# A four-network graph kernel: last attention summed by blocks and sources, GpSimd's low parts in halves, first products read in PSUM, one later spread

## The reference

```
def gat_layer(x, W, a_s, a_d, b, edge_index, concat):
    h = (x @ W).reshape(n, H, C)
    alpha_s = jnp.einsum('nhc,hc->nh', h, a_s)
    alpha_d = jnp.einsum('nhc,hc->nh', h, a_d)
    e = jax.nn.leaky_relu(alpha_s[src] + alpha_d[dst], NEG_SLOPE)
    m = jax.ops.segment_max(e, dst, num_segments=n)
    e = jnp.exp(e - m[dst])
    denom = jax.ops.segment_sum(e, dst, num_segments=n)
    msg = h[src] * (e / (denom[dst] + EPS))[:, :, None]
    return jax.ops.segment_sum(msg, dst, num_segments=n) + b
...
x = _layernorm(x + _L0_gnn_ref(x, ...), axis=-1)
```

## Time and profile before

| what | us |
|---|---|
| median of 3 runs | 1843.94 (1842.36 to 1847.01) |
| the profiled execution | 1845.62 |
| its span in the trace | 1843.8 |
| PE busy | 1777.4 (96%) |
| DVE busy | 1226.3 (67%) |
| ACT busy | 718.9 (39%) |
| POOL busy | 701.7 (38%) |

### The profile page before, as it was taken

One profiled execution on the slowest core, in us unless ns is written; L12 is line 12 of the kernel. 1 busy time (PEld: TensorE's weight loads), 2 busy tenths in 40 slices (PEclk: granted clock), 3 DMA queues, 4 the chain that ended last, 5 costly groups with the idle time before them and its releaser, 6 DMA issues. The chain is left out here.

```text
span 1843.8 us, 26174 instructions
## 1 busy us (share of the span) xinstructions
PE 1777.4 (96%) x8953; PEld 1488.6 (81%) x8953; DVE 1226.3 (67%) x2214; ACT 718.9 (39%) x1166; POOL 701.7 (38%) x388
## 2 busy tenths in 40 slices
PE   8999899999999999998999899899999999999998
PEld 3444587999999999877986698887887888899977
DVE  9999687888878878666758856775224222444556
ACT  0112645454454444433366644333224222433131
POOL 1556341423424323211667775522233333332321
PEclk9999999999999999998999999999999999999999
DMA  1000642212212224103320032312222223223231
GB/s 21 1 23 34 248 147 61 95 52 95 93 54 95 84 63 146 52 26 126 107 68 1 1 106 70 100 58 64 74 89 77 77 86 89 89 78 90 89 129 51
DMA packets 54206, 143.23 MB, mean 78 GB/s; under 512 B 13780, under 2 KB 13908, under 8 KB 53076
## 3 DMA queue, kind: packets, MB, share of 16 engines
q1 hardware_dynamic: 47332, 108.48, 18.9%
q10 hardware_dynamic: 6768, 33.30, 5.0%
HBM read 129.18 MB, written 12.58 MB: 77 GB/s over the span
## 5 line engine op out<-in xcount | busy, mean ns | idle before, releaser
L767 POOL TENSOR_TENSOR w_pair<-early,w_pair 128x768 fp32r<-128x768 f32 x234 | 446.4, 1936 | 877.5 <-ACT w_pair L1469 877.4
L851 PE MATMUL ps<-w_pair,cols_x 128*128 128x384 f32 x2088 | 377.2, 338 | 0.6 <-DVE al_part L1891 0.6
L851 PEld LDWEIGHTS ps<-w_pair,cols_x 128*128 128x128 f32 x2088 | 364.0, 189 | 5.9 <-issue 3.4
L851 PE MATMUL ps<-w_pair,wide 128*128 128x384 f32 x1872 | 334.8, 339 | 4.4 <-DVE wide L1882 3.1
L851 PEld LDWEIGHTS ps<-w_pair,wide 128*128 128x128 f32 x1872 | 328.9, 190 | 9.6 <-DVE wide L1882 5.0
L1469 ACT ACTIVATE w_pair<-early 128x768 fp32r<-128x768 f32 x234 | 181.4, 840 | 314.4 <-PE ps L851 146.4
L1404 PE MATMUL ps<-wide,w_pair 128*128 128x512 f32 x972 | 226.5, 392 | 2.8 <-DVE wide L1882 2.8
L1404 PEld LDWEIGHTS ps<-wide,w_pair 128*128 128x128 f32 x972 | 181.2, 188 | 42.0 <-DVE wide L1882 5.2
L436 PE MATMUL count_ps<-early,src_hot 128*128 (+1 forms) x816 | 180.1, 384 | 7.7 <-DVE early L356 7.6
L436 PEld LDWEIGHTS count_ps<-early,src_hot 128*128 (+1 forms) x816 | 80.4, 99 | 106.9 <-issue 10.4
L356 DVE TENSOR_SCALAR early<-node_f,edge_f,weight 128x512 f16 x204 | 148.2, 776 | 0.0
(11 more groups left out here) (277 smaller groups left out, 2421.7 us busy)
## 6 DMA issues: line engine op xcount, KB each, us to landing
early<-weights SPq DMA_DIRECT2D x240, 384.0 KB, 3.1
edge_mask<-counts ACTq DMA_DIRECT2D x13, 512.0 KB, 3.2
multi<-attn ACTq DMA_DIRECT2D x8, 768.0 KB, 4.6
kept<-early ACTq DMA_DIRECT2D x3, 1536.0 KB, 6.0
counts<-out SPq DMA_DIRECT2D x7, 512.0 KB, 2.6
multi<-kept ACTq DMA_DIRECT2D x2, 1536.0 KB, 7.4
edge_mask<-masks ACTq DMA_DIRECT2D x5, 512.0 KB, 3.3
last_raw<-weights SPq DMA_DIRECT2D x6, 384.0 KB, 6.3
```

The lines of the kernel that those rows point to most:

```text
L767: return nc.gpsimd.tensor_tensor(dst, whole, high.bitcast(F32), ALU.subtract)
L851: mm = nc.tensor.matmul(ps[:, m, 0:HW], left[:, a, k, m * P:(m + 1) * P], w_pair[:, slot_of[0], b, k, :], start=(k == 0 and a + b == 0), s ...
```

## The change

**1. POOL's low parts of weights.** `weights_low` makes two subtractions of 128x384 in place of one of 128x768, for every part of every pass; the semaphore is raised by the second.

**2. First products read in PSUM.** For the tiles of head 0 and head 1 (passes 0 to 3) ACT makes only the rounded copy, and DVE reads bank m itself in its three operations (`direct`). PE then waits for `rows_ready` (DVE is done with the bank) in place of `tile_copied` before it writes the bank again.

**3. Small steps of head 0 one tile later.** In head 0 the transposition of `kc`, its spread, ACT's copy of it and DVE's `small_uv` each stand one product tile later.

**4. The first network's last attention.** A new `block_sums` takes three half tiles (tile 0 left and right, tile 1 left) by sources, in banks 2, 3 and 6, and the other five one after the other in banks 7, 0, 1, 2, 3. `block_norm` replaces `norm`: for each tile of nodes its own variance term, root and normalization. The wait for the relational weights (`wk_hi` 2) moves from ahead of everything to before the first use of bank 0. The residual and bias have a place of their own (`first_resid`, in the memory of `wide1`), are loaded when the last head has been summed, and are added before the probabilities' last part is waited for. The third relation's code becomes a call of `block_sums` with two half tiles by sources, which gives the same instructions as before.

**5. The later spread.** In the first relational `row_sums` the spread of the last source terms stands after the first right half tile in place of before it.

```diff
+FIRST_BANK = (2, 3, 6, 7, 0, 1, 2, 3)
+FIRST_SIDE = 3
...
-                    low_of(w_pair[:, slot, 1, 2 * p:2 * p + 2, :], w_raw[:, p],
-                           w_pair[:, slot, 0, 2 * p:2 * p + 2, :]).then_inc(w_low, 1)
+                    whole = w_raw[:, p]
+                    low_of(w_pair[:, slot, 1, 2 * p, :], whole[:, 0], w_pair[:, slot, 0, 2 * p, :])
+                    low_of(w_pair[:, slot, 1, 2 * p + 1, :], whole[:, 1], w_pair[:, slot, 0, 2 * p + 1, :]).then_inc(w_low, 1)
...
-                            product(j_rows, m, cols_x, tile_copied, h * 8 + (4 + m + 1))
+                            product(j_rows, m, cols_x, rows_ready if h < 2 else tile_copied, h * 8 + (4 + m + 1))
...
-                        if u == 0:
+                        if u == (0 if with_last else 1):
                             pe.wait_ge(kc_ready, h + 1)
...
+            def block_sums(source, weights_of, x_base, banks, side, before_tile, small=()):
+                for i in range(side):
+                    before_tile(i)
+                for s in range(NB):
+                    pe.wait_ge(x_lo, x_base + s + 1)
...
+                    for i in range(side):
+                        m, n = i // 2, i % 2
...
+                for i in range(side, 2 * NB):
+                    m, n = i // 2, i % 2
+                    before_tile(i)
...
+            def attention_tile(i):
+                if i < 2:
+                    pe.wait_ge(acc_added, 69 + FIRST_BANK[i])
+                elif i == 4:
+                    pe.wait_ge(wk_hi, 2)
+                elif i >= 6:
+                    pe.wait_ge(row_read, i - 6 + 1)
...
-            pe.wait_ge(wk_hi, 2)
-            row_sums(rows[0], prob, 80, acc_added, 69, 0, {2: turn_last_weights})
+            block_sums(rows[0], prob, 80, FIRST_BANK, FIRST_SIDE, attention_tile, {2: turn_last_weights})
...
-            row_sums(rows[0], prob_sets[0], 140, tile_copied, 109, 8, {2: last_source, 3: spread_last_source}, dotted=85)
+            row_sums(rows[0], prob_sets[0], 140, tile_copied, 109, 8, {2: last_source}, dotted=85, late=spread_last_source)
...
-                copy(hv[:, m % 2], ps[:, m, 0:HW])
+                if not direct:
+                    copy(hv[:, m % 2], ps[:, m, 0:HW])
                 copy(dst[:, 0, m, n * HW:(n + 1) * HW], ps[:, m, 0:HW]).then_inc(tile_copied, 1)
...
+            act.wait_ge(agg_done, KB * HEADS0)
+            act.dma_start(resid0, x).then_inc(res_in, 16)
...
-                tile = hv[:, m % 2]
+                tile = ps[:, m, 0:HW] if direct else hv[:, m % 2]
...
+            add_bias_to_residual(0, resid0, b_row0)
             dve.wait_ge(x_lo, 84)
...
-            norm(attention_rows)
+            block_norm(0, attention_rows, order=BLOCK_ORDER)
```

126 lines of the change are left out of this document (59 added, 67 removed).

## The result

The changed kernel took 1828.12 us (median of 4 runs, 1826.29 to 1830.05), beside 1843.15 us for the kernel before on the same chip. The ratio is 0.9904, with a 95% interval of 0.9884 to 0.9925: 17.7 us less (13.8 to 21.4). Run again later on another occasion, it had the ratio 0.9921 (0.9902 to 0.9940), 14.6 us less (11.1 to 18.1). The forecast was 12.4 us less, 1831.5, in a range from 1828.0 to 1838.5. The medians of the first measurement are only 15.0 us apart, so its four runs alone place the gain no better than within some 3 us.

What follows compares the result with a forecast made beforehand. PE, busy 96% of the span, was taken to bound the kernel, so only its waits pay. Terms 4.9 + 5.6 + 1.2 + 0.7 = 12.4 us take the median from 1843.94 to 1831.5, range 1828.0 to 1838.5.

Steps and rivals of the forecast that it cites:

- First products: Head 0, edits 2 and 3: the 3.10 us wait before `kc` and 1.8 us of low clock go, 4.9 us.
- just in time: Head 0, small terms' transposition: DVE has them ready at 266, PE reaches it at 266.8, so no new wait.
- Halves: POOL's low parts, edit 1: shorter DVE holds remove the 1.22 us wait before a last relational attention `kc`, 1.2 us.
- Last attention: First network, edit 4: start 0.8, middle 2.15, end 1.8 and clock 0.8 us, together 5.6, bounds 3 and 6.4.
- if DVE keeps up. It does: Last attention's end: DVE's 3.47 us per block fits PE's 4.3 us, so three other tiles' 1.8 us go.
- the low clock that might go: Last attention, after its first gap, shrinking from 2.0 to 1.2 us: about 1.6 us of clock loss, half counted, 0.8.
- Later spread: Last relational attention, edit 5: PE resumes at 1167.8 in place of 1168.46, 0.7 us, bounds 0 and 2.4.
- The wait did not move on in head 0: Rival at head 0's small terms: they come 3 to 5 us late, gap and clock loss reappear, about 1836; chance 0.16.
- Halves did collect somewhere else: Rival: halves hold DVE's chains as long, small waits of 0.3 to 1 us arise at several places, 1838 to 1843; chance 0.12.
- The slower case: Rival at the small terms in 7 heads: six POOL holds outlast the slack, 1858 us; chance 0.05.
- The clock's case: Three open places where avoided or split gaps move time up to 3 us either way, 1828.5 to 1834.5; 0.67 with the forecast.
- The sign at the turning: Last attention's end: the trace after should show one wait of 2.5 to 3 us inside the first four transposes.

Runs made afterwards that it cites:

- the one with quarters: The changed kernel with POOL's weight low parts in four operations of 128x192 instead of two of 128x384: 1835.51 us, ratio 0.9942.
- The three kernels with five filled waits: Changed kernel, unread products in five PE waits: three half tiles by sources 1825.88 us; two 1826.82; two, with the last turning's twelve products moved ahead of DVE's last row 1822.62.
- Late halves alone: The kernel before with halves only in the loop for the last passes (from pass 46 on, the convolution): 1838.83 us, ratio 0.9976.
- The run with filled waits: The changed kernel with eight unread products of 128x384 in PE's wait ahead of the last attention: 1826.68 us, ratio 0.9909.
- two half tiles beside the sources: The changed kernel with two half tiles instead of three by sources in the last attention, so six follow: 1832.80 us, ratio 0.9939.

## Why the prediction was off

**First products: 4.9 predicted, 5.0 in the trace.** The wait of 3.10 and the low clock behind it went, as said. Also the small terms were "just in time" as predicted, without a bracket. Edits 2 and 3 alone gave 6.5 us (4.1 to 8.9), which holds the term. The steps fit too: none of DVE's reads of the eight tiles was held (0.55 to 0.61 us each, which is also what a read of SBUF took when POOL did not hold it; before, five had taken 1.4 to 2.2), `kc` was there at 246.30 (246.4 predicted), and PE wanted it at 249.78. What the forecast did not say is that, by these rows, either edit would have done. PE was through with its ninth tile at about 246.7, so with the reads in PSUM alone `kc` was in time; and `kc` as it came before, at 249.80, would have met a PE that asks at 250.0. No run separates the two. The stretch behind it, 290.38 to 739.28, has only two values in all traces, 447.3 to 447.4 and 448.9 to 449.0 us, and each occurs with the edits and without: one low clock, which is there or not. In two executions with the edits PE waited 0.5 us at 231 us for `al_part`, at the bank that was called the tightest, and in the one with quarters 0.8 us at 221 for POOL.

**Halves: 1.2 predicted, 5.5 in the traces. This is the term that failed.** The wait before `kc` went as predicted (57.93 to 57.97 us without halves, 56.58 to 56.62 with them, in every trace). But the sentence "What it changes is how long DVE is held" was followed to this one place, and POOL's work counted as something "for whose weights PE never waits". PE did wait for DVE's results that POOL held, in the convolution. The waits stood in the trace of before (5.6 us at L1341). The convolution takes 504.6 to 504.9 us with whole operations (five traces) and 501.4 to 501.9 with halves (eight), 3.1 less, and the last part 1.1 less. The three kernels with five filled waits have halves too and took 502.3 to 503.9, with more low clock there in two of them. Late halves alone gave it all.

**Last attention: 5.6 predicted, 2.7 in the pair of traces, 2.5 on average.** The start gave 0.7 (0.8 predicted) and the middle 2.15, as said. The end gave 1.2 instead of 1.8. PE's last sum ends 7.85 us before the first product, and ended 9.08 before. The failed step there is "if DVE keeps up. It does". The 3.47 us of DVE for a block were held against PE's 4.3, but three half tiles lie ready at once when the denominators are read: eight tiles take DVE 842.78 to 856.7, PE is done at 853.5. The larger miss is the clock. I had counted 0.8 for the low clock that might go. Instead 6.8 us of it followed on the gap of 1.29 us, where before 3.4 followed on 2.01. From the first denominators to the last sum, waits left out, PE took 24.36 us (829.15 to 853.51) and before 23.01 (836.66 to 861.82, less 2.15): 1.35 us lost and not 0.8 won. The pair is no accident: in six traces with three half tiles and nothing filled in, 6.8 to 13.7 us of low clock followed on the 1.29, in six without the edit 3.4 to 10.2 on the 2.01. That the 1.22 us gap of the relational part was followed by none was no guide to this place, where products of two columns stand between the others; that these make the difference is not shown. The run with filled waits shows the size: 3.3 us. In sum, 0.7 + 2.15 + 1.2 - 1.35 = 2.7.

**Later spread: 0.7 predicted, nothing measured.** The trace pair shows 2.03 us less, which would be easy to book to this edit. Ten traces with it (nothing filled in at these sums) took 65.6 to 68.0 us for that stretch, mean 66.8, and five without 66.0 to 67.9, mean 67.1; alone its ratio was 1.0004. The step that failed is that the 2.78 us gap of one trace was taken to stand in every execution. Sorted by the low clock between the 1.88 us wait ahead of the second source and the spread, the traces agree:

| low clock ahead of the spread, us | without the edit: wait, stretch | with it: wait, stretch |
|---|---|---|
| none | 2.78, 67.6 (2 traces) | 2.15, 65.6 (1) |
| 3.4 | 1.18, 66.0 (1) | 0.55 to 0.59, 65.6 (3) |
| 6.8 | none, 66.3 (1) | none, 66.3 (1) |
| 10.2 | none, 67.9 (1) | none, 67.9 to 68.0 (5) |

A low clock ahead of the wait eats it, and then the edit has nothing to shorten. Only where none stood did the edit show the 2 us, most of it the low clock that followed on the 2.78.

**The sum.** With the terms as the traces have them it is 5.0 + 2.5 + 5.5 + 0.2 = 13.2 us, and by timed runs of the parts 13.6: two misses, one too low by 4.3 and one too high by 3.1, nearly cancelled. The second measurement, 14.6, agrees with that. The first, 17.7, is higher by 4 and its interval reaches down to 13.8. In the profiled pair the other 5.4 us goes with the clock: PE lost (1 - 0.986) x 1843.8 = 25.8 us of full-clock time before and (1 - 0.989) x 1825.2 = 20.1 after, 5.7 less, of which the first products (1.8 won) and the last attention (1.35 lost) have 0.45. So 5.25 us lie where no term of the forecast stood. It took both, the halves' missing 4.3 us and this clock, to carry the first measurement past the range; without either it would have stayed inside. Whether the changed kernel has a better clock as a rule or had it in those runs stays open; in the later runs it had 0.986 to 0.991.

**The rivals and the signs.** The wait did not move on in head 0: the small terms were there at 265.34 us and PE wanted them at 266.48. Halves did collect somewhere else, but as a gain. The slower case named a half of about 1.2 us as the point from which it decides, and the prediction says that one above it would prove it wrong. That sign appeared and meant nothing: of the 468 halves 72 took more than 1.2 us, 32 of them from 300 to 740 us, the longest 1739 ns, and yet PE had no idle time from 300 to 720 us and no bracket at the small terms of any head. In head 1 they were ready at 328.04 and wanted at 329.26, with the 1.2 us of slack that was there before. The length of 48 other operations (median 1017) had been no guide to these. The clock's case allowed 3 us either way at three places; in the pair it was 5.4, and it lay mostly at places that the case did not count. The sign at the turning, one wait of 2.5 to 3 us, was missed as well: there were two, 1.02 and 2.37.

## What to carry to other kernels

When a change shortens what one engine is held by another, list every instruction of the held engine that stands beside the holder, in all stages, and ask of each who waits for it. A search for the waits of the critical engine in each stage costs one view and would have shown the 5.6 us. Two edits that each might remove the same wait want a run each, or a look at when the awaited value was ready. Before a gain in a pair of traces is booked to an edit, lay the same stretch of all traces side by side, with and without it: here one stretch moved by 2 us for no reason of the edit. And a wait that can't be removed can be filled with work that nobody reads, provided it stands ahead of the wait that really ends last.

## What the runs showed of the hardware

- A VectorE subtraction with both inputs in SBUF was held over five GpSimd operations in a row (2.81 us for one of 0.69), when these were 128x192 and followed each other without a gap; 19 others beside such operations took 0.81 to 1.13 us. With 128x384 it took 1.18 at the same place, with 128x768 1.92.
- A GpSimd subtraction takes 1851, 1019 and 601 ns (medians) for 768, 384 and 192 columns: each more operation costs near 0.19 us.
- A gap of 1.29 us in TensorE's work was followed by 6.8 us at the lower clock (6.8 to 13.7 in six traces), and with two half tiles beside the sources by 17.1 us; a gap of 1.22 was followed by none elsewhere. With products that nobody reads in the same gap the clock stood at 1.00 from 825 to 837 us.
- The low stretches fall at other places from one execution to the next of the same kernel. The stretch of before from 739.28 to 819.55 us, in which only edit 1 lies, took 78.5 to 78.7 us in eleven traces and 80.1 to 80.3 in seven, and nothing between; both values occur with halves and with whole operations.
